# Fused attention and FFN kernel: row vectors folded into the channel-major state, the residual x by a second DMA, new orders on each engine

## The reference, cut to what matters

```python
xn = _layernorm(x)                                  # (8, 1024, 256)
return x + attn(xn) + ffn(xn)

def attn(xn):                                       # 16 heads of depth 16
    q, k, v = heads(xn @ Wq + bq), heads(xn @ Wk + bk), heads(xn @ Wv + bv)
    q, k = elu(q) + 1, elu(k) + 1
    k = k / sqrt(sum(k * k, -1) + EPS)
    out = merge((q @ k.T) @ v) @ Wo + bo            # no softmax
    y = xn + out
    return (y - mean(y)) / sqrt(var(y) + EPS) * gamma + beta

def ffn(xn):
    h = xn
    for blk in range(3):                            # i0, i1 = 2 * blk, 2 * blk + 1
        y = qlora_linear(h, i0)                     # 4 bit codes * scale, + bias, + low rank part
        y = gelu(layernorm(y) * ln_gamma[blk] + ln_beta[blk])
        h = h + qlora_linear(y, i1)
    return h
```

## Time and profile before

| | before |
|---|---|
| median of 3 runs | 634.25 us (634.12 to 634.41) |
| profiled execution | 636.37 us |
| its span | 634.6 us (1.77 us lie around it) |
| mean granted TensorE clock | 0.983 |
| TensorE busy | 602.0 us (95%) |
| VectorE busy | 498.5 us (79%) |
| ScalarE busy | 446.8 us (70%) |
| GpSimd busy | 414.2 us (65%) |
| DMA | 20.88 MB, mean 33 GB/s |

### The profile page before, as it was taken

How to read it: one execution, slowest core, us unless ns; L and a number is a source line. 1 busy time by engine, 2 the same in 40 slices (tenths; PEclk the granted TensorE clock), 3 DMA queues, 4 the chain that set the end, 5 groups by cost and what they waited for, 6 DMA issues and landing times.

```text
span 634.6 us, 10275 instructions
## 1 busy us (share of the span) xinstructions
PE 602.0 (95%) x3357; PEld 515.6 (81%) x3357; DVE 498.5 (79%) x1079; ACT 446.8 (70%) x699; POOL 414.2 (65%) x361
## 2 busy tenths in 40 slices
PE   7999999899998999989998999989999899989996
PEld 6888879788887888878787888878888787877875
DVE  2678689787888869788797868887787886978578
ACT  2558876858678586786778776784967857777653
POOL 3766766676476756757477674867667585765664
PEclk9999999899998999989999999989999899999999
DMA  8201001200021000300002000120002000010001
GB/s 239 71 3 34 33 1 41 93 1 2 1 99 33 0 0 0 132 0 0 0 33 99 0 0 0 71 61 0 0 0 106 26 0 0 0 67 1 1 1 67
DMA packets 9442, 20.88 MB, mean 33 GB/s; under 512 B 2367, under 2 KB 4302, under 8 KB 9422
## 3 DMA queue, kind: packets, MB, share of 16 engines
q1 hardware_dynamic: 8944, 20.22, 9.5%
q10 hardware_dynamic: 478, 0.41, 0.2%
HBM read 12.24 MB, written 8.39 MB: 33 GB/s over the span
## 4 chain that ended last, share of the span: by engine, by line
PE 51%; DVE 16%; ACT 12%; POOL 10%; issue 7%; DMA 2%; DVEq 0%; POOLq 0%; ACTq 0%; SPq 0%
PE bank L1427 14%; PE bank L1554 9%; PE bank L1433 7%; PE bank L1565 6%; PE bank L1527 3%; POOL sqs L404 3%; ACT fw L614 2%; POOL XNB L399 2%; DMA out_dram<-RES 2%; DVE Y L1030 2%; PE bank L1606 2%; DVE RES L1036 2%; POOL rsf L368 2%; DVE Y L1010 2%; PE bank L1519 2%
## 5 line engine op out<-in xcount | busy, mean ns | idle before, releaser
L253 POOL TENSOR_TENSOR gl<-fw,gh 128x512 fp32r<-128x512 f32 x80 | 102.6, 1298 | 55.9 <-ACT gh L619 55.8
L404 POOL TENSOR_TENSOR sqs<-fw 128x512 f32<-128x512 f32 x48 | 61.8, 1287 | 51.0 <-ACT fw L604 50.8
L604 ACT ACTIVATE fw<-bank,b1c 128x512 f32<-128x512 f32 x96 | 61.6, 683 | 46.4 <-PE bank L1433 46.2
L614 ACT ACTIVATE fw<-fw,vec 128x512 f32<-128x512 f32 x96 | 74.9, 808 | 9.7 <-DVE fw L935 9.4
L935 DVE SCALAR_TENSOR_TENSOR fw<-bank,b1c,rb 128x512 f32<-128x512 f32 x96 | 68.2, 744 | 10.7 <-ACT rb L610 10.7
L368 POOL TENSOR_TENSOR rsf<-vef,neghalf 128x4 f32<-128x4 f32 x48 | 51.6, 1074 | 33.8 <-DVE vef L928 31.3
L258 POOL TENSOR_TENSOR hTl<-hT,hTh 128x512 fp32r<-128x512 f32 x40 | 57.9, 1468 | 16.4 <-ACT hTh L623 16.3
L1554 PE MATMUL bank<-K,XN 128*128 128x256 f32 x256 | 61.9, 379 | 0.0
L610 ACT ACTIVATE rb<-bank 128x512 f32<-128x512 f32 x48 | 28.6, 595 | 45.3 <-PE bank L1527 45.3
L1598 PE MATMUL bank<-M,qT 128*128 128x256 f32 x256 | 59.4, 379 | 0.0
L368 POOL TENSOR_TENSOR rs<-ve,neghalf 128x2 f32<-128x2 f32 (+1 forms) x48 | 39.7, 835 | 29.9 <-DVE ve L1021 18.5
(11 more groups left out here) (148 smaller groups left out, 1681.1 us busy)
## 6 DMA issues: line engine op xcount, KB each, us to landing
X<-in_L_attn_x_dram SPq DMA_DIRECT2D x16, 512.0 KB, 3.7
out_dram<-RES SPq DMA_DIRECT2D x14, 512.0 KB, 2.6
XNB<-in_L_ffn_qweights_dram SPq DMA_DIRECT2D x2, 512.0 KB, 7.4
out_dram<-RES SPq DMA_DIRECT2D x4, 256.0 KB, 2.1
RES<-in_L_ffn_qweights_dram SPq DMA_DIRECT2D x1, 512.0 KB, 6.3
Y<-in_L_ffn_lora_a_dram ACTq DMA_DIRECT2D x4, 96.0 KB, 7.6
Wp<-in_L_attn_Wq_dram SPq DMA_DIRECT2D x1, 256.0 KB, 4.9
Wp<-in_L_attn_Wk_dram SPq DMA_DIRECT2D x1, 256.0 KB, 5.2
```

The lines of the kernel that those rows point to most:

```text
L253: engine.tensor_tensor(gl[:, h, m, :], fw[:, h, m, :], gh[:, h, m, :].bitcast(F32), ALU.subtract).then_inc(g_low[h][m], 1)
L404: pool.tensor_tensor(sqs[:, h, :], fw[:, h, 0, :], fw[:, h, 1, :], ALU.add).then_inc(sqs_ready[h], 1)
L604: act.activation(fw[:, h, m, :], FB[h][m][:], ACT.Square, bias=b1c[:, m, j:j + 1]).then_inc(sq_ready[h], 1)
L614: act.activation(fw[:, h, m, :], fw[:, h, m, :], ACT.Gelu, bias=lnb[:, m, j:j + 1], scale=lng[:, m, j:j + 1]).then_inc(g_ready[h], 1)
```

## The change

1. `base_x`, `beta_sum`, beta_r and b5_r are gone. RES is filled with x by a second DMA, `load_res`, on SP: in the head behind the weights' use of that memory, in a body and the tail behind the store of the same half. It covers half a batch, 512 KB, and there are two per batch. `att_result` waits for it (res_loaded). `next_x` now waits for the normalisation (xn_ready), which has read X.
2. beta is loaded as a thirteenth row of vec_rows. `bias_last` adds beta and the last bias (shift) to column NL-3 of vec, the bias of the second block's second layer, so that they enter hT with the residual of block 1 and go through to the output. Since block 2 then reads a shifted state, `shift_sums` (TensorE, eight small matmuls) and `bias_shift` (VectorE) take the weight's product with the shift out of b1c of block 2. Both run once, in the head.
3. `base_xn` works on pairs, four pieces per batch of 256 tokens, instead of two halves.
4. The orders of the head, body and tail on all engines are new, as are HEAD_USES and BODY_USES.

The core of the diff:

```diff
+NVEC = 2 * NBLK + 2 * NBLK + 1
...
+            def load_res(i, h, at):
+
+                if at == HEAD:
+                    if h == 0:
+                        sp.wait_ge(wT_high, NL)
+                else:
+                    sp.wait_ge(stored[h], 16 * i)
+                sp.dma_start(RES[:, h * HT:(h + 1) * HT, :],
+                             x_rows[bass.ds(i, 1), :, h * HT:(h + 1) * HT, :].rearrange("o p t d -> (o p) t d")
+                             ).then_inc(res_loaded[h], 16)
+
             def next_x(i, h):
 
-                sp.wait_ge(x_based, nth(i, 2, h))
+                sp.wait_ge(xn_ready, nth(i, NT, h * HT + HT - 1))
                 load_x(i + 1, h)
...
             def body(i):
+                load_res(i, 0, BODY)
+                load_res(i, 1, BODY)
                 next_x(i, 0)
                 next_x(i, 1)
                 store(i, 0)
                 store(i, 1)
...
-            def base_x(i, h, at):
-
-                pool.wait_ge(xn_ready, nth(i, NT, h * HT + HT - 1))
+            def base_xn(i, p, at):
+
+                pool.wait_ge(xn_ready, nth(i, NT, 2 * p + 1))
                 if at == HEAD:
-                    pool.wait_ge(rows_ready, 1)
-                    pool.wait_ge(wT_high, NL)
+                    pool.wait_ge(w_row, 32)
+                    pool.wait_ge(wT_high, p + 1)
                 else:
-                    pool.wait_ge(stored[h], 16 * i)
-                pool.tensor_tensor(RES[:, h * HT:(h + 1) * HT, :], X[:, h * HT:(h + 1) * HT, :],
-                                   beta_r[:].unsqueeze(1).broadcast_to([P, HT, D]), ALU.add).then_inc(x_based, 1)
...
+                    pool.wait_ge(y_ready, nth(i - 1, NT // 2, p))
+                pool.tensor_tensor(XNB[:, 2 * p:2 * p + 2, :], XN[:, 2 * p:2 * p + 2, :],
+                                   bo_r[:].unsqueeze(1).broadcast_to([P, 2, D]), ALU.add).then_inc(xn_based, 1)
...
             def body(i):
-                base_x(i, 0, BODY)
                 add_squares(i, 0, 0)
-                base_x(i, 1, BODY)
                 ffn_root(i, 0, 0)
+                base_xn(i, 0, BODY)
                 add_squares(i, 1, 0)
-                base_xn(i, 0, BODY)
                 ffn_root(i, 1, 0)
+                base_xn(i, 1, BODY)
...
                 dequantise(3)
+                base_xn(0, 0, HEAD)
+                qk_lower(1)
                 dequantise(4)
                 dequantise(5)
                 add_squares(0, 0, 0)
-                base_xn(0, 0, HEAD)
                 ffn_root(0, 0, 0)
-                qk_lower(1)
...
             def att_result(i, p, at):
 
-                dve.wait_ge(x_based, nth(i, 2, p // 2))
+                dve.wait_ge(res_loaded[p // 2], 16 * i + 16)
...
+            def bias_last():
+
+                dve.wait_ge(vecs_ready, 2)
+                dve.tensor_tensor(shift[:], vec[:, :, NVEC - 1], vec[:, :, NL - 1], ALU.add).then_inc(shift_ready, 1)
+                dve.wait_ge(shift_ready, 1)
+                dve.tensor_tensor(vec[:, :, NL - 3], vec[:, :, NL - 3], shift[:], ALU.add).then_inc(shift_ready, 1)
...
+            def shift_sums():
+
+                r = take(0, ("shift",), HEAD)
+                pe.wait_ge(wT_split, NL - 1)
+                pe.wait_ge(shift_split, 2)
+                pairs = [(k, w) for k in range(NC) for w in (WTl, WTh)]
+                for m in range(NC):
+                    for n, (k, w) in enumerate(pairs):
+                        ins = pe.matmul(RB[r][:, 2 * m:2 * m + 2], w[:, NL - 2, k, m * P:(m + 1) * P], shiftr[:, k, :],
+                                        start=(n == 0), stop=(n == len(pairs) - 1))
+                ins.then_inc(rot_full[r], 1)
...
                 spread_rstd(i, 1, 0, BODY)
+                project_q(i, 1, 0, BODY)
                 project_q(i, 0, 0, BODY)
                 project_q(i, 0, 1, BODY)
-                project_q(i, 1, 0, BODY)
...
                 gelu(i, 0, 0, 0)
+                gelu(i, 0, 0, 1)
+                k_square(i, 2)
                 g_higher(i, 0, 0, 0)
-                gelu(i, 0, 0, 1)
+                k_square(i, 3)
+                g_higher(i, 0, 0, 1)
                 rb_copy(i, 1, 0, TAIL)
-                g_higher(i, 0, 0, 1)
-                k_square(i, 2)
-                k_square(i, 3)
```

355 lines of the change are left out of this document (185 added, 170 removed), and 14 rows, old and new, of tables (BODY_USES, HEAD_USES).

## The result

The changed kernel took 640.47 us (median of 4 runs, 640.15 to 640.95), the kernel before 634.18 us (4 runs, 633.34 to 634.41). The ratio is 1.0102, with a 95% interval of 1.0085 to 1.0120: slower by 6.3 us, outside the range of the prediction (630.0 to 637.0), and the third case of the forecast (slower), which had 23%.

What follows compares the result with a forecast made beforehand. TensorE, busy 95% of the span, was taken as the bound, its stall a round trip through VectorE and GpSimd, not GpSimd's load. Bodies 0, head +0.4, tail +0.1 gave +0.5 on 634.25: 634.8 us, range 630.0 to 637.0.

Steps and rivals of the forecast that it cites:

- third case of the forecast: Whole kernel: the outcome slower, against faster 0.36 and same 0.41; chance 0.23.
- The bodies: Six loop turns: removing base_x leaves TensorE's stall at 2.2 to 2.3 us, so cost 0.
- Every sign that the prediction named: Bodies' profile: base_x gone, GpSimd near 375 us, wait of 2.2 to 2.35 before half 1's spread, GpSimd idle before last root.
- rival 3: Bodies: GpSimd's squares of half 1 late, +0.35 us per body, +2.1 in all, 636.9; 13%.
- The base line: Whole kernel: median of runs 634.25, taken as 2.12 us below the profiled execution, with +0.5 added.
- Rival 2: Bodies: stall stays but some keep the clock, 1.59 us each; one 633.2, two 631.6, three 630.0; 33%.
- The size of a kept clock: Bodies, behind the spread: five projection pairs take 2.30 us with the clock up against 3.89, so 1.59 per body.
- rival 1: Bodies: the stall was GpSimd's queue and goes with its slow clock, 6 x 3.93 = 23.6 us, 611.2; 4%.
- The head: Before the first body: shift_sums adds 0.79, the 0.4 wait for vec goes, net +0.4; bounds -0.8 and +1.5.
- sign of being wrong: Profile after: prediction wrong if, among others, the first body starts over 1.5 us away from before's.
- Nearly gapless, so its length is the sum of its work: Head on TensorE: few gaps, so only added and removed work counts; the 14 fillers, 0.89 us each, just change places.
- The tail: After the last body: base_x removed, ScalarE's rb_copy of half 1 later; +0.1 us, bounds -0.6 and +1.0.

Runs made afterwards that it cites:

- a_samepos: The changed kernel with 1952 unused bytes ahead of X, putting X and all behind it at the addresses of the kernel before: 635.78 us, ratio 1.0008.
- a_oldorders: The changed kernel with the orders of the kernel before on all engines: 641.21 us, ratio 1.0112.
- b_stallfill: The kernel before with two filler groups between turn_squares and spread_rstd of half 1, block 0, in the bodies: 627.73 us, ratio 0.9877.
- b_moredma: The kernel before with x loaded once more in each body, 384 KB a half, into memory nobody reads: 634.40 us, ratio 1.0009.
- a_reorder: The changed kernel with project_k(i, 3) moved between turn_squares and spread_rstd of half 1, squares before the first base_xn, reduction two places earlier: 641.59 us.
- a_stallfill: The changed kernel with two filler groups between turn_squares and spread_rstd of half 1, block 0, in the bodies: 634.69 us.
- b_pad128: The kernel before with 128 unused bytes ahead of X: 636.60 us, ratio 1.0033.
- b_again: The kernel before, unchanged, measured and profiled again for a second trace: 634.47 us.
- a_smalldma: The changed kernel with the second load of x cut from 512 KB to 32 KB a half in bodies and tail: 640.47 us.
- a_oldhead: The changed kernel with only the head's orders taken from the kernel before: 639.87 us.
- b_pad32: The kernel before with 32 unused bytes per partition ahead of X: 636.39 us, ratio 1.0025.

## Why the prediction was wrong

**The bodies: mechanism right, a term missing.** Every sign that the prediction named for them was there: base_x gone, GpSimd at 374 us, a wait of 2.2 to 2.35 behind the root, idle GpSimd ahead of it. I costed the bodies at 0, with -0.6 as the lower and 2.1 as the upper bound; they cost 1.08 in the trace. The cause is none that the prediction weighed. It is not the squares (rival 3), though these did come late. Counted from `turn_squares` of half 0, they ended at 5.15 us (the prediction has 5.11), `turn_squares` of half 1 took another 0.15 to start, and so it came at 5.28 to 5.30 in every kernel with the new order on GpSimd and the key projection in its place, at 5.01 to 5.22 with the old one. With the fast stream one sees it in the gap ahead of it (TensorE, a_samepos; the squares ended at 194.62):

```profile
194.25 0.39 PE L1576 MATMUL bank<-Wqkh,xTl 128*128 128x256 f32 x2
194.77 0.63 PE L1552 MATMUL bank<-ident,sqs 128*128 128x128 f32 x4
197.58 1.04 PE L1560 MATMUL bank<-ident,rsf 128*128 128x128 f32 x4 [2.18 <-POOL rsf L385]
```

But the spread, which ends the stall, did not follow the squares. It came at 8.09 in the kernel before and at 8.10 in this row, and at 8.22 in the changed kernel and in a_oldorders, both at the shift of -1952, the one with the new and the other with the old order on GpSimd. These 0.13 us per body, 0.8 of the 1.08, go with the place in SBUF: VectorE's key products wait for ScalarE's exponentials of the key projections, which the slower matmuls deliver later (the last of these products ahead of the reduction starts at 4.24 us instead of 4.11), and VectorE's reduction stands behind them. The step that failed is that a matmul which is not moved costs what it did. I compared orders and queues and read the removal of two tensors as freed memory; the operands of some 70 us of TensorE's work per body moved with it.

**The base line.** "The median of the runs, 634.25, is 2.12 below the profiled one, so 634.25 + 0.5" carried the difference over as if it were a constant of measuring. The traces put it down to the clock, in two places. In the bodies it was an execution in which the stalls cost it everywhere, against a median in which, by the spans and clocks of the others, it stayed up in one or two. At the start the first 32 filler matmuls took 6.53 us, the longest of all traces with that head, and the first body started at 113.78; in b_stallfill, where nothing ahead of the bodies differs, the chain has

```profile
3.46 5.35 PE bank L1606 x32
```

and the first body started at 112.66. Between 6.7 and 9.0 us TensorE was busy throughout in both and did 13 matmuls in the one, 20 in the other. Rival 2 rested on the same error: "Before, all six lost the clock, so a change can only give". The median of before had kept clocks to lose, and the changed kernel lost them. Its picture of an edge in the length of the stall does not hold either: b_moredma kept the clock behind a stall of 2.49 us in its first body, and a_samepos lost it behind one of 2.18 in its second. The base line is some 2.5 of the 6.3 us: 2.12 subtracted, and the changed kernel's median 0.3 above its profiled execution. The spans and granted clocks of several executions would have shown this; one profile could not.

**The size of a kept clock.** 1.59 us was read from five pairs of matmuls. A whole body gains 1.3 in the kernel before (74.85 to 73.53) and 0.9 to 1.0 in the changed one, since ScalarE and VectorE are nearly as late. In rival 1, at 23.6 us, that part was mis-sized in the same way: the fillers gave 6.5 us in the kernel before (634.2 to 627.7) and 5.8 in the changed one. Its other part, the stall itself, was never removed cleanly: a_reorder took away stall and slow clock both and gave nothing, but made ScalarE late by its own edit.

**The head.** Forecast +0.4, upper bound +1.5, measured +2.17, which is also the prediction's own sign of being wrong (a first body over 1.5 us away). shift_sums cost what it was put at (0.79). The rest is mostly idle time: 1.35 us for XN at the start and 0.97 for the squares of half 1 in block 2:

```profile
11.66 0.63 PE L1452 MATMUL bank<-ident,XN 128*128 128x128 f32 x4 [1.35 <-ACT XN L603]
...
97.29 0.30 PE L1551 MATMUL bank<-ident,sqs 128*128 128x128 f32 x1 [0.97 <-POOL sqs L409]
```

I had counted the fillers as work that only changes places. Two of them were what TensorE did until XN was there; moved behind it, they leave it idle for 1.35 us and are still to be done. And 2.17 flatters the change, since it is taken against the slowest start of the kernel before, whose first body started at 112.66 to 113.78 in the traces with its head. The changed head gives such a faster start away: `qk_sums` behind the first fillers took 2.80 us in a_stallfill, 2.23 in the changed kernel and 1.96 in a_samepos, TensorE then waited 0.85, 1.35 and 1.55 us for XN, and the first body started at 116.03, 115.95 and 115.62. Against the fast starts (b_stallfill, b_pad128) the head costs 3 us. "Nearly gapless, so its length is the sum of its work" is true of a trace and not of a reordered program.

**The tail.** Forecast +0.1, measured +0.54. The wait of 0.83 us for hTh did vanish, but so did the clock behind the stall at 574.20. It vanished in b_again too, without any change, where the clock fell there as well.

**The sum.** With the clock held up by fillers the two kernels can be compared without its steps: 634.69 against 627.73, 6.96 us. One step after the other took off 1.41 (32 bytes), 2.74 (ScalarE's order) and 1.21 (the rest of the way to the old addresses); 1.60 stay, with a first body that starts 3.06 us later (115.72 against 112.66), bodies that are 0.2 us shorter than those of b_stallfill and a tail 0.4 us shorter. So at the old addresses the forecast of 634.8 would have been 1.0 us off (635.78), but in part by luck: the head cost up to 3 us instead of 0.4, and the bodies, forecast at 0, got shorter. Without fillers the addresses alone take off 4.7 of the 6.3 us. That is more than the bodies' 0.3 us each: in the trace of a_samepos two bodies and the tail kept their clock. Why the clock fell in every body of the changed kernel is not settled. The slower stream alone is not the reason: a_smalldma kept it in two bodies and a_oldhead in one at the shift of -1952, and b_pad32 in two at 75.2 us for the rest.

## What to carry to other kernels

A change to the list of buffers moves every operand behind it: pin the layout, or pad it back, before anything else of a change is judged, and compare the start-to-start distance of matmuls that were not touched. Put TensorE's own filler into a stall that can't be shortened; here two filler groups per body made the kernel before 1% faster (634.2 to 627.7 us) and its four times steady. Before real work is moved into a stall instead, find out who waits for its result. And before a profiled execution serves as the base of a sum, compare its clock and span with those of a few other executions.

## What the runs showed of the hardware

- TensorE's matmul stream depended on where in SBUF its operands lie: pairs of 512 columns at 0.459 or 0.467 us, pairs of 256 at 0.229 or 0.236 to 0.240, with nothing changed but an unused tensor ahead of them. The 1952 bytes were worth 4.7 us in this kernel (640.47 against 635.78). Single bodies of one execution also differed at the same addresses (0.227 and 0.236 in b_pad128).
- 0.8 MB more of DMA per body beside the matmuls did not slow them by anything that could be measured (b_moredma, 0.228 to 0.229 us as before, ratio 1.0009), nor did 1.0 MB less speed them up at unchanged addresses (a_smalldma, 0.240).
- The granted clock fell to 0.50 behind stalls of 2.2 to 2.5 us in some bodies and not in others of the same execution, the longer stall not being the surer one (kept behind 2.49 us in b_moredma, lost behind 2.18 us in a_samepos), and with 1.8 us of such a stall filled it fell in hardly any (mean clocks of 0.996 to 1.000).
- At the start the same 32 filler matmuls took 6.53 us in one trace and 5.35 in another (before, b_stallfill), and the first body moved with them, from 113.78 to 112.66.
